# First chunk: four tiles of small tables looked up by one-hot matmuls, and a landing wait behind each four gathers

## The reference

```python
e = jnp.stack([tbl_0[ids[:, 0]], ..., tbl_39[ids[:, 39]]], axis=1)   # (2048, 40, 64)
p, q = e[:, rowidx], e[:, colidx]                                    # all pairs i < j
z = jnp.einsum('bie,fie,bif->bi', p, param, q)                       # (2048, 780)
h = jnp.concatenate([z, dense_ctx], axis=1)
h = jnp.maximum(h @ W_top1 + b_top1, 0.0)                            # 796 -> 512
h = jnp.maximum(h @ W_top2 + b_top2, 0.0)                            # 512 -> 256
y = h @ W_top3                                                       # 256 -> 1
```

## Time and profile before

| | |
|---|---|
| median of three runs | 1405.21 us (1401.72 to 1406.98) |
| the profiled execution | 1401.97 us, span 1400.2 us |
| PE busy | 1260.3 us, 90% |
| ACT busy | 1029.3 us, 74% |
| DVE busy | 990.6 us, 71% |
| POOL busy | 606.1 us, 43% |

### The profile page before, as it was taken

How to read it: one execution, slowest core, us unless ns; L and a number is a source line. 1 busy time by engine, 2 the same in 40 slices (tenths; PEclk the granted TensorE clock), 3 DMA queues, 4 the chain that set the end, 5 groups by cost and what they waited for, 6 DMA issues and landing times.

```text
span 1400.2 us, 23412 instructions
## 1 busy us (share of the span) xinstructions
PE 1260.3 (90%) x5952; PEld 535.6 (38%) x5952; DVE 990.6 (71%) x1615; ACT 1029.3 (74%) x7945; POOL 606.1 (43%) x646
## 2 busy tenths in 40 slices
PE   1124879699999999999999999999999999999999
PEld 0002333244444444444344444444343444444343
DVE  0104777478988778778888778777888778688880
ACT  0003668486864889889995889889996799899981
POOL 7774553655322555555523555555414565000000
PEclk9756788799999999999999999999999999999999
DMA  4111121222221222222212222122211222111100
GB/s 163 26 26 39 45 65 40 57 53 64 60 67 53 56 56 66 65 65 65 66 46 58 66 68 65 43 66 66 75 48 44 66 67 65 47 46 47 40 2 0
DMA packets 31840, 77.78 MB, mean 56 GB/s; under 512 B 11924, under 2 KB 12436, under 8 KB 31576
## 3 DMA queue, kind: packets, MB, share of 16 engines
q1 hardware_dynamic: 11088, 55.12, 12.2%
q0 software_dynamic: 20480, 21.01, 7.4%
q10 hardware_dynamic: 136, 0.14, 0.1%
HBM read 76.22 MB, written 0.01 MB: 54 GB/s over the span
## 4 chain that ended last, share of the span: by engine, by line
PE 78%; ACT 9%; another core or an unknown queue 8%; issue 5%; DVE 1%; ACTq 0%; DVEq 0%
PE ring L607 34%; PE z_ps L630 16%; PE ring L612 15%; ACT wide_prod L457 8%; PE ring L636 7%; PE ring L582 3%; PE ring L640 1%; ACT e_t L418 1%; DVE prod L522 1%; PE ring L643 1%; DVE wide_prod L535 0%; PE ring L589 0%; ACT z_t L430 0%; ACT L418 0%
## 5 line engine op out<-in xcount | busy, mean ns | idle before, releaser
L457 ACT ACTIVATE wide_prod<-wide_prod 128x64 f32<-128x64 f32 x3904 | 934.0, 242 | 62.9 <-issue 36.3
L402 POOL DMA_INDIRECT rows<-tbl,idx_now x640 | 605.4, 946 | 582.6 <-DMA rows<-tbl,idx_now 215.1
L522 DVE TENSOR_TENSOR prod<-ring,e_t 128x512 f32<-128x512 f32 x1008 | 628.8, 682 | 262.4 <-PE ring L607 103.6
L457 ACT ACTIVATION_READ_ACCUMULATOR wide_prod<-wide_prod 128x1 f32 x3904 | 738.3, 189 | 37.6 <-issue 36.9
L607 PE MATMUL ring<-e_t,w 64*128 64x512 f32 x2176 | 615.3, 623 | 63.8 <-issue 39.4
L535 DVE TENSOR_TENSOR wide_prod<-ring,rows 128x512 f32<-128x512 f32 x512 | 328.1, 682 | 101.9 <-PE ring L612 74.9
L607 PEld LDWEIGHTS ring<-e_t,w 64*128 64x128 f32 x2176 | 260.5, 191 | 342.6 <-issue 210.1
L612 PE MATMUL ring<-w,e_t 64*128 64x512 f32 x1024 | 321.7, 633 | 40.7 <-DVE prod L519 24.7
L630 PE MATMUL z_ps<-prod,strip 128*32 128x512 f32 x2096 | 253.1, 595 | 0.2
L612 PEld LDWEIGHTS ring<-w,e_t 64*128 64x128 f32 x1024 | 119.7, 192 | 172.0 <-issue 81.3
L418 ACT ACTIVATE e_t<-ring 128x512 f32<-128x512 f32 x80 | 45.8, 587 | 168.7 <-remote 87.8
(11 more groups left out here) (17 smaller groups left out, 31.9 us busy)
## 6 DMA issues: line engine op xcount, KB each, us to landing
w<-weights SPq DMA_DIRECT2D x64, 768.0 KB
rows<-tbl,idx_now POOLq DMA_INDIRECT x640
w<-weights SPq DMA_DIRECT2D x4, 512.0 KB
w<-w1z SPq DMA_DIRECT2D x1, 1792.0 KB
w<-w2p SPq DMA_DIRECT2D x1, 512.0 KB
idx_now<-idx SPq DMA_DIRECT2D x4, 80.0 KB
z_t<-dense_t ACTq DMA_DIRECT2D x8, 16.0 KB
y_out_dram<-h ACTq DMA_DIRECT2D x4, 2.0 KB
```

The costliest lines, as they stand in the source:

```text
L402: nc.gpsimd.indirect_dma_start(out=rows[:, slot, t, E * f:E * f + E], out_offset=None, in_=tables[m * 2 + f], in_offset=bass.IndirectOffse ...
L457: last = nc.scalar.activation(products, products, ACT.Copy, accum_out=z_b[:, h, t, col:col + 1])
L522: nc.vector.tensor_tensor(dst[:, j, :], ring[:, bank, :], e_t[:, k, :], ALU.mult).then_inc(t_free, 1)
```

## The change

In chunk 0 tiles 4 to 7 are no longer gathered. Eight fields with tables of 1000 rows (3, 4, 14, 15, 19, 25, 29, 30) are moved to places 8 to 15, so that they make up these four tiles; the matrices and first-layer weights are dealt accordingly (`FIELD_AT`). SP loads the eight whole tables, 125 partitions of eight rows each, and ACT issues eight loads that copy the field's 512 ids of chunk 0 to 125 partitions (256 KB each, both kinds). They stand in `z_t`, `h1` and `h2`. For each of the eight rows per partition (j) and each field (h) DVE compares the ids with the row number, `(ids - 8p) == j`, into one of eight halves of `wide_prod`, and PE multiplies the table's slice (125 x 64) with that 0/1 block (125 x 512); the sixteen matmuls of a tile add up in one bank what `transpose_tile` would have put there.

The tiles of chunk 0 are now brought up in the order 4, 0, 5, 1, 6, 2, 7, 3, 8, 9, ...; `T_NUMBER` gives the count that the semaphores reach. `prep_at` puts tiles 4 to 7 where 0 to 3 stand, and from 8 on m items ahead. POOL gathers tiles 0 to 3, 8, 9, ... and waits for the landing behind each four gathers in chunk 0 too, except behind the very first four. The later chunks gather all their tiles as before.

```diff
+ONE_HOT = (4, 5, 6, 7)
+SMALL = (3, 4, 14, 15, 19, 25, 29, 30)
+HOT_P, HOT_J = 125, 8
+HOT_AT = {0: (4, 5), 1: (6,), 3: (7,)}
+FIRST_TILES = [4, 0, 5, 1, 6, 2, 7, 3]
...
     if c == 0:
+        if m in ONE_HOT:
+            m -= ONE_HOT[0]
         first = FIRST_OF[0, max(m, 1)]
-        return first if m < 5 else first - 2 if m < 10 else first - m
+        return first if m < ONE_HOT[0] else first - m
...
+            def load_tables(i):
+                for h in range(2):
+                    pos = 2 * ONE_HOT[i] + h
+                    sp.dma_start(hot_table[2 * i + h], tables[pos].rearrange("(p j) e -> p (j e)", j=HOT_J)
+                                 ).then_inc(hot_in[i], 16)
+
             load_idx(0)
+            for i in range(2):
+                load_tables(i)
             load(0)
-
-            sp.wait_ge(transposed, 1)
+            for i in range(2, len(ONE_HOT)):
+                load_tables(i)
+
+            sp.wait_ge(transposed, T_NUMBER[0] + 1)
...
-            for tile in range(ALL_TILES):
+            for tile in GATHERED:
...
-                    if c > 0:
+                    if c > 0 or m > 0 or f > 0:
 
                         pool.wait_ge(gathered[slot], 16 * BT * (f + 1 + 2 * (use - 1)))
...
+            for i in range(len(ONE_HOT)):
+                for h in range(2):
+                    q = 2 * i + h
+                    act.dma_start(hot_idx[q], hot_ids[q:q + 1, :].broadcast_to([HOT_P, NB])).then_inc(hot_in[i], 16)
...
+            def one_hot(tile):
+                i = ONE_HOT.index(tile)
+                dve.wait_ge(hot_in[i], 4 * 16)
+                for j in range(HOT_J):
+                    for h in range(2):
+                        number = (i * HOT_J + j) * 2 + h
+                        if number >= len(hot):
...
+                        nc.vector.tensor_scalar(hot[number % len(hot)], hot_idx[2 * i + h], first_row_f[0:HOT_P, :],
+                                                float(j), ALU.subtract, ALU.is_equal).then_inc(hot_ready, 1)
...
             for n, (c, kind, i) in enumerate(ITEMS):
+                for tile in HOT_AT.get(n, ()):
+                    one_hot(tile)
...
+            def look_up_tile(tile):
+                i = ONE_HOT.index(tile)
+                dst = take_bank(("tile", tile))
+                pe.wait_ge(hot_in[i], 4 * 16)
+                for j in range(HOT_J):
+                    for h in range(2):
+                        number = (i * HOT_J + j) * 2 + h
+                        pe.wait_ge(hot_ready, number + 1)
+                        last = nc.tensor.matmul(dst[E * h:E * h + E, :], hot_table[2 * i + h][:, E * j:E * j + E],
+                                                hot[number % len(hot)], start=j == 0, stop=j == HOT_J - 1)
+                        if (j, h) != (HOT_J - 1, 1):
+                            last.then_inc(hot_used, 1)
+                last.then_inc(transposed, 1)
```

More of the change, by code:

```diff
@@ L240, in last_reader @@
                if (m in UNITS[i] or UNITS[i] == (m + 1, m + 1) if kind == "unit" else m == WIDES[i][0]))
+TILE_ORDER = FIRST_TILES + list(range(len(FIRST_TILES), ALL_TILES))
+T_NUMBER = {tile: n for n, tile in enumerate(TILE_ORDER)}
+GATHERED = [tile for tile in range(ALL_TILES) if tile not in ONE_HOT]
 TILES_AT = {}
-for _t in range(ALL_TILES):
+for _t in TILE_ORDER:
     TILES_AT.setdefault(prep_at(_t), []).append(_t)
@@ L285, with bilinear_tower @@
 BANKS, BEFORE = bank_plan()
-def bilinear_tower(nc, tables, idx, dense_t, weights, w1z, b1c, w2p, b2c, w3c, out):
+def bilinear_tower(nc, tables, idx, hot_ids, dense_t, weights, w1z, b1c, w2p, b2c, w3c, out):
     with ExitStack() as ctx:
@@ L396, in _ @@
                 elif use > 1:
-                    pool.wait_ge(transposed, max(t for t in range(tile) if slot_of(t)[0] == slot) + 1)
+                    last = max(t for t in GATHERED if t < tile and slot_of(t)[0] == slot)
+                    pool.wait_ge(transposed, T_NUMBER[last] + 1)
                 for f in range(2):
@@ L594, in bilinear @@
                 if FIRST_OF[c, m] == n:
-                    pe.wait_ge(e_ready, c * TILES + m + 1)
+                    pe.wait_ge(e_ready, max(T_NUMBER[c * TILES + k] for k in range(m + 1)) + 1)
                 piece, o = WEIGHT_PLACE[c, kind, i]
```

58 lines of the change are left out of this document (45 added, 13 removed).

## The result

| | time, us | against before |
|---|---|---|
| before | 1403.47 (1399.93 to 1406.98, 4 runs) | |
| the changed kernel | 1318.82 (1318.43 to 1326.37, 4 runs) | 0.941, 95% interval 0.9367 to 0.9452 |
| its profiled execution | 1318.43, span 1316.6 | 83.6 us less span |

A forecast was written before the change was run, and what follows sets the result against it. The end was taken to be set by when PE reaches its dense part, delayed by slow stretches under unbroken gathers. A (opening, 8 us) plus B (rows 3 to 12, 69 us) gave 1402 - 77 = 1325 us, range 1295 to 1366.

The forecast's parts named there:

- What bounds it, and the mark: PE's dense part starts at 280 us and sets the end; mark: tile 14's transposes (item 84), 276.94 before, near 197 after.
- A long unbroken run of gathers starves the other engines, and a pause lets them catch up: Before 280 us: PE's 1.4 us per instruction and ACT's and DVE's "issue" idling come from POOL's unbroken gathers; pauses cure them.
- Term B: Rows 3 to 12, up to item 84: 199 us before, 130 after, 69 us saved (39 to 82).
- 108 + 5, plus 17 for waits on PE and ACT: Rows 3 to 12 without slow stretches: DVE work of 108 + 5 us plus 17 of waits, 130 us.
- Term A: The opening up to row 3: a serial chain of 70 us against 78 before, 8 us saved (-4 to 20).
- The loads: Opening: eight tables and eight id rows, 4.1 MB; all landed near 13 us at best, tile 4's start taken as 12.
- The gathers: Chunk 0: 16 tiles instead of 20, 6.45 us per four gathers, tile 19 landed near 210 us, slack for later tiles.
- After item 84: From tile 14's transposes to the end: PE stays full, cost zero.
- More is gained: Opening 58 us by fast compares or warm lookups, rows 3 to 12 at DVE's floor: 102 us saved, 1300 us; chance 0.18.
- Pauses don't cure: The slow stretches before 280 us persist despite POOL's pauses: A 0 or less, B 39, about 1363 us; chance 0.14.
- Slower: Opening: lookups fall into a slow stretch, 5.6 us each instead of 0.6; 32 of them give 1485 us; chance 0.05.
- No change: PE's slow stretch just moves and eats both savings, opening and rows 3 to 12: 1402 us; chance 0.04.

The follow-up runs named there:

- waits alone: The kernel before with only the landing waits of chunk 0 added: 1334.52 us (1.0413) on chip 8, 1337.46 us (0.9621) on chip 0.
- job 2: Group of runs on chip 0, before at 1403.96 us: the changed kernel again, 1329.49 us, and its table loads split over all DMA engines, with and without waits.
- late wait: The kernel before, POOL waiting in chunk 0 behind tile m's gathers for tile m-1's landing: 1282.75 us (1.0001) on chip 8, 1392.29 us (1.0008) on chip 0.
- bare pause: The kernel before, POOL filling scratch four times behind each four gathers of chunk 0: 1328.57 us (1.0357) on chip 8, 1339.69 us (0.9642) on chip 0.
- waits-from-tile-8 kernel: The changed kernel with loads spread over all DMA engines and chunk 0's landing waits only from tile 8 on: 1322.16 us (0.9511) on chip 0.
- all-engine loads: The changed kernel with table loads split into 112 and 13 partitions and ids copied to 128: 1322.83 us (0.942); without chunk 0's waits 1403.53 us.
- lookups alone: The changed kernel with its landing waits of chunk 0 taken out, on chip 8: 1282.41 us, 0.9998 of before.

## Why the prediction was right, and where its terms were off

By the time, 1318.8 against 1325, on a chip with slow steps; on one like chip 8 the same forecast would have had the wrong sign (the estimate above). By its steps:

- **What bounds it, and the mark.** Right. 85.4 us at tile 14 became 83.6 us of span. The stretch from tile 14's transposes to the last tile's is nearly the same: 1036.1 us before, 1038.2 after, 1037.0 with the waits alone. It isn't exact: in all kernels on chip 0 it lies between 1031 and 1045, and for the changed kernel it was 1044.9 in job 2.
- **"A long unbroken run of gathers starves the other engines, and a pause lets them catch up".** Right for chip 0. That the pauses cure is shown: taking the waits away brings the 5.6 us steps back (1403.5 us, in the kernel with the loads on all engines), adding only them takes them away (0.962), a late wait doesn't (1.001), a bare pause does (0.964). That the others are starved of instructions stayed an argument from the even steps, and run and rate aren't told apart. What it did not say, and no row of one profile could, is that the starving belongs to the chip: on chip 8 there was none, and the waits alone cost 4%.
- **Term B**, forecast 69 with the floor at 82, measured 80. The mis-sized step is "108 + 5, plus 17 for waits on PE and ACT". In the 119 us DVE is busy 108.8 us (the windows from 72 to 192 us), 4 less than the 113, and 10 us are left for waits and not 17. Both the DVE work and the waits were put too high, and together they are the 11 us by which B was missed. PE's clock was counted against it, and was 1.00 there: with the slow steps the reduced clock of the earlier trace rows went too.
- **Term A**, forecast 8 (-4 to 20), measured 5. That it came so close is luck: its parts were off in both directions. The lookups started at 16.17, not 12. A compare repeats every 0.40 us (16 in 6.42), not 0.60, so a tile costs 10.1 us for the first and 7.1 to 7.4 for the others, instead of 9.6 for each. And the transposes waited 6.2, 4.5 and 0.7 us for tiles 1, 2 and 3, a wait that the sum did not have: the "up to 6 us" for landing behind the loads went into the landing times once and not into the sum, but it comes with each wait, 4.51, 4.39, 6.51 and 5.70 us before POOL may go on. So the start cost 4 us more, the gathers 11 more, the lookups 6 less (32.0 instead of 38.4), and the 4 us for slow stretches fell away. Nor was PE's clock near full from 20 us on, as the prediction's last paragraph expected: it was 0.76 from 40 to 60 us, around PE's waits of 6.2 and 4.5 us for gathers, and the transposes there took 1.12 us instead of 0.66.
- **The loads.** For the sixteen the row of the trace gave 13 us at best and my choice for tile 4 was 12; the last of tile 4's landed at 15.5. The windows show 143 to 174 GB/s at half use, and with the loads laid out anew 291 to 306 at full use. By the rule of the Trainium skill (DMA: Bandwidth & Descriptors, Why a DMA increments its semaphore by 16) 125 partitions go over 5 engines, and the trace agrees: from 15.5 to 20 us, with little else under way, the 16 DMA engines are busy by three tenths (5 of 16 are 0.31) at 119 to 139 GB/s. The estimate from it gave 11 us for the start, which left out what else was in the queues. Of the six us that the spread loads won at the start, 2.4 were left at tile 3.
- **The gathers.** Forecast 6.45 us for each four, tile 19 near 210; measured 7.0 on average (tile 8's last gather goes out at 81.9 us, tile 19's at 235.2, eleven tiles of two groups behind it). Tile 14's last went out at 168, 23 us before its need, so the slack held, with less of it than the 50 us of the forecast.
- **After item 84**: zero forecast, 2 us given back, with PE busy 80.00 of the 80 us from 200 on.

**The rivals.** *More is gained*: half of it came about. The compares were faster and B came within 2 us of its floor, but the late gathers took it back in the opening. *Pauses don't cure*: refuted on chip 0; the standstill at 265 us, which went on behind a pause, fits the waits-from-tile-8 kernel, in which the steps shrink in the second pause, not at once. Its doubt from the Trainium skill (Runtime: NRT & Kernel Launch, Instruction fetch mechanics), that crossing a block is mostly hidden, isn't contradicted: the stretch starts at 20 records of PE's matmuls in one kernel and at 80 in another, so it isn't one block's end that brings it, and in the middle of it the instruction queues move nothing (below). *Slower*: its mechanism is real (the compares 5.6 us apart), and the waits are what keeps the kernel out of it. *No change*: it is nearly what the lookups do without the waits, which on chip 0 was measured with the all-engine loads only (1403.5 against 1404.0).

**Which part earns what on chip 0.** The waits alone take 52 us (1389.7 to 1337.5). The rest, between 8 and 19 us by the two measurements of the changed kernel, comes from the lookups, which relieve the slower gathers; the two were measured in other jobs than the waits alone, and the 1% between jobs is as large as this share. With the all-engine loads it is 1322 to 1323, in the same job 0.5% below the changed kernel. No version is known to be best on both chips: of the four kernels run on chip 8 none beat the kernel before, and neither the changed kernel nor the all-engine loads ran there.

## What to carry to other kernels

Look at the engines' steps beside long runs of gathers: if products or copies come at an even 5.6 us although they last 0.7, break the run behind each four gathers for 1.7 to 1.9 us; a landing wait and a fill of scratch memory did equally well here. First see whether the chip shows the steps at all, by measuring the unchanged kernel on more than one, since the pause costs what it takes where there is nothing to cure. Count a landing wait at the price it has among the transfers that it will meet (4.4 to 6.5 us here beside the opening's loads, 2.3 on average beside the weights, 1.7 alone), once for each wait on the path.

## What the runs showed of the hardware

- **Two chips differed by 8 to 9% on one kernel**: 1282.7 us in one job on chip 8 against 1390 to 1404 us in three on chip 0 for the kernel before, and 0.2% apart with a landing wait behind each four gathers. The difference reaches into the later chunks, where POOL waits behind each four anyway: from tile 14's transposes to the last it is 1016.4 and 1015.9 us on chip 8 (lookups alone, late wait; 1026.2 with the waits alone, whose chunk 1 waits for tiles) and 1031 to 1045 us in every kernel on chip 0. ACT's "issue" waits in its sums from 280 to 600 us are 12.3 us in the changed kernel on the slower sort of chip (3 to 14 in the others there); on chip 8 the profile lists none. So four gathers in a row seem to leave some 20 us of the slowness; that is read from the profile and not tested with shorter runs.
- **What the slowness is stays open.** It comes after 30 to 45 us of unbroken gathers, in a weaker form also with runs of eight and 1.7 us between them; an instruction of PE then takes 1.4 us whatever its size, ACT and DVE are slowed too, and it ended within two short pauses. It is not the number of gathers in flight, not their landing and not a fixed place of the instruction streams. It isn't a lack of DMA bandwidth either. In the kernel before, the queues of the profile from 50 to 100 us, in the midst of it, have one row only, the gathers' (packets, MB, share of the 16 engines):

```profile
q0 software_dynamic: 1276, 1.31, 13.5%
```

That is 26 GB/s. The instruction queues, which the page lists for the whole run, moved nothing in that time while PE worked on at its slow steps. Whether it is the supply of instructions that is slow, and why one chip has it and another not, no run shows.
- **Compares hold up the gathers.** On chip 8, in the kernel with the lookups and no waits, DVE's timeline has

```profile
37.81 6.42 DVE L609 TENSOR_SCALAR wide_prod<-h,first_row_f 125x512 f32<-125x512 int32 x16 [0.32 <-DMA z_t<-tbl]
```

and POOL's beside it

```profile
37.43 0.99 POOL L443 DMA_INDIRECT rows<-tbl,idx_now  x1 [0.30 <-issue]
38.73 1.28 POOL L443 DMA_INDIRECT rows<-tbl,idx_now  x1 [0.30 <-issue]
40.31 1.28 POOL L443 DMA_INDIRECT rows<-tbl,idx_now  x1 [0.30 <-issue]
41.89 2.47 POOL L443 DMA_INDIRECT rows<-tbl,idx_now  x1 [0.30 <-issue]
44.66 0.94 POOL L443 DMA_INDIRECT rows<-tbl,idx_now  x1 [0.30 <-issue]
```

A gather's issue takes 1.28 and 2.47 us instead of 0.94 and is back to that when the compares end; four gathers took 7.2 us instead of 5.0. That is 2.2 us for this tile's compares. By the Trainium skill (SBUF — State Buffer, Who interferes with whom) DVE in one of its two-port modes and GpSimd lock each other out of a shared pair of ports for a whole instruction; the trace agrees. The compare's 0.40 us, against 0.60 for a product, also leans to the fast mode that the Trainium skill (VectorE: DVE Perf Modes, Mode 2×_2P) names for an operation with one source; the prediction's estimate for it was 0.33.
